# A fused hybrid layer on one core: projections loaded and turned in thirds, the two folds in a row, another order of the attention stage

## Chip, core and metric

One core of one Trainium2 chip. The metric is the device time of one execution in microseconds; the median of three executions is 124.89 us (124.87 to 124.93). The core's engines are TensorE (PE; its weight loads are listed as PEld), VectorE (DVE), ScalarE (ACT), GpSimd (POOL) and SyncE (SP), which here only issues DMAs. Each works through its own queue in order and they meet only through semaphores.

## The reference, cut to what matters

The input x is 2 x 512 x 256, float32. Four blocks follow one another, each with a residual:

```python
x = x + attn_a(layernorm(x), qkv, o_proj, gamma, beta)   # itself: layernorm * gamma + beta, q, k, v,
                                                         # causal softmax(q k^T / 16) v, o_proj, + residual
x = x + ffn(layernorm(x), gate_w, up_w, down_w, scales)  # weights rounded to fp8; silu(gate) * up, then down
x = x + s4d(layernorm(x), D, log_dt, A, C)               # a convolution over 512 steps with a complex kernel
x = x + ffn(layernorm(x), ...)                           # the same weights again
```

## The kernel before

The 1024 rows of x are eight tiles of 128 rows: tiles 0 to 3 are the first batch, 4 to 7 the second. The program is one hand-written list per engine; there is no planner, and the order in each list is the order of the work.

**The opening, 0 to about 28 us.** TensorE fills its time with transposes of the identity matrix (`warm_up`, 14 of them, L1099), turns the q third of `qkv` when it has landed (`turn_w`, L1107), does 8 more identity transposes, and turns the k third. It turns the parameter rows (L1148), turns the first two normalised tiles (`turn_z`, L1122), and multiplies the turned q and k thirds into one 256x256 matrix `wqk` (`fold`, L1114). It turns tiles 2 and 3 and the v third, and makes g = xn wqk for the whole first batch (`make_g`, L1131: eight passes of 512 columns). Only then comes the second fold, `wvo` = v o_proj, then the turning of the second batch, v rows for the first batch (`make_v`, L1138: sixteen passes of 256 columns), `scores(0)` (L1173), the turning of the scales (L1230), `make_g(1)`, `scores(1)`, `turn_probs(0)` (L1186) and `make_v(1)`.

Each product has to be copied from PSUM before TensorE can use it: ScalarE copies the turned thirds (L505), `wqk` and `wvo`, and half of xn, g and v; VectorE the other half. xn needs gamma and beta, which `params` holds, read by VectorE from the turned parameter rows. `normed` is made by VectorE for the first batch (L739) and by ScalarE for the second (L540); the reciprocal standard deviations are GpSimd's (L296, L301, L306).

ScalarE's list also has one tanh and one sine group for the convolution's taps, the squares of the gate and up weights (L558) and the exponentials. An activation of another table set is preceded by an ACT_TABLE_LOAD.

**Attention, to 51.9 us.** For k = 2 to 7, TensorE does `scores(k)`, `attend(k-2)` (L1198), `turn_probs(k-1)`. VectorE takes each row maximum (L892), ScalarE the exponential (L578) and the copy of the turned probabilities (L586), VectorE the division and residual (L900) and the statistics. Between these stand VectorE's work on the three fp8 grids (L811, L816) and on the down weights (`lift_down`, `lower_down`), and GpSimd's rounding of the gate and up weights (`round_weight`, L413 and L416), the factors of x_plus (`x_plus_scales`, L400 to L404), the reciprocal deviations of the new x, the first and middle part of the taps, and the six tiles of `down16` (L446).

**Four passes of the feed-forward part.** In each, TensorE does 6 steps `gate_up(n, m)` (L1258) and, three steps later, `down(n, m)` (L1292); `spread_taps` (L1303) stands in pass 0 after step 4, and `copy_taps` (L629) on ScalarE brings its result to SBUF before `turn_h(1, 0)` may write the same PSUM bank.

**DMA order on SP (L243 to L256):** x tiles 0-1, q, x tiles 2-3, k, four parameter rows, v, x tiles 4-5, 6-7, o_proj, two scale rows, gate, up, down, down_scale. ScalarE issues three small loads, GpSimd two (c_re, c_im).

Of the kernel before, what the change touches and what calls it, by code (L numbers as in the profile page):

```python
# [34 lines left out]
WARM_UP = 14  # L35
WARM_BETWEEN = 8
# [9 lines left out]
def hybrid_layer(nc, x, qkv, o_proj, gamma, beta, d_param, log_dt, a_real_log, a_imag, c_re, c_im,  # L46
# [13 lines left out]
    with ctx:  # L60
# [48 lines left out]
        param_rows = sb("param_rows", [4 * C, P])  # L109
        params = sb("params", [P, 4 * C])  # L110
        gammas, betas, log_dts, d_params = (params[:, C * n:C * n + C] for n in range(4))
# [33 lines left out]
        q_loaded, k_loaded, v_loaded, wo_loaded = sem("q_loaded"), sem("k_loaded"), sem("v_loaded"), sem("wo_loaded")  # L145
# [83 lines left out]
        def _(sp):  # L229
# [25 lines left out]
            load_chunks(down_raw[:], down_w, w_loaded[2])  # L255
            sp.dma_start(down_scale_all[:], down_scale.partition_broadcast(P)).then_inc(down_scale_loaded, 16)  # L256
# [16 lines left out]
        def _(pool):  # L273
# [11 lines left out]

            def load_s4d(n, array, loaded):
                pool.dma_start(s4d_in[:, n, :].rearrange("p (c n) -> p c n", c=C),
                               array.rearrange("(c p) n -> p c n", p=P)).then_inc(loaded, 16)
# [97 lines left out]
            def constants():  # L386

                load_s4d(2, c_re, c_loaded)
                load_s4d(3, c_im, c_loaded)
# [58 lines left out]
            inverse_std(1, T, 2, negative_mean=True)  # L448
            taps_middle()
            inverse_std(1, T + 2, 2, negative_mean=True)  # L450
            taps_end()
# [18 lines left out]
            for n in range(2 * B):  # L470
# [19 lines left out]
                else:  # L490
                    tail(n, POOL_TAILS[n][0])
                    if n == 3:
# [9 lines left out]
        def _(act):  # L502
            def turned(w):
# [4 lines left out]
            def xn_chunk(b):  # L508
                act.wait_ge(params_ready, 1)
                act.wait_ge(z_turned, C * b + 1)  # L510
                act.activation(xn_cols[:, b, 0, :], psum[:, BANK_Z[b][0], :], ACT.Identity, scale=gammas[:, 0:1],
                               bias=betas[:, 0:1]).then_inc(xn_by_act, 1)

            def g_part(b):
                act.wait_ge(g_made, C * b + 1)
                act.activation(g_cols[:, b, 0, :], psum[:, BANK_G[b][0], :], ACT.Copy,
# [6 lines left out]

            act.dma_start(e_in[:, 0:HN].rearrange("p (c n) -> p c n", c=C),
# [9 lines left out]
            act.wait_ge(wqk_made, 1)  # L534
            act.activation(wqk[:].rearrange("p c n -> p (c n)"), psum[:, BANK_WQK, :], ACT.Copy).then_inc(wqk_ready, 1)
            xn_chunk(0)
            turned(2)
# [4 lines left out]
            act.wait_ge(wvo_made, 1)  # L542
# [828 lines left out]
```

## Time and profile before

| | |
|---|---|
| median of 3 runs | 124.89 us (124.87 to 124.93) |
| the profiled execution | 124.83 us, of which the span from first to last instruction is 123.0 us |
| PE busy | 116.2 us, 94% of the span |
| DVE, POOL, ACT busy | 96.1, 83.7, 77.5 us |
| granted TensorE clock, mean | 0.995 |

The page lists busy time by engine; the chain of waits follows the work back from the last instruction; a timeline lists instructions in order of time, each with the idle time of its engine before it and what ended that. Every number of the argument is from the one profiled execution. A matmul's listed duration holds its way through the array; the next one of an unbroken row starts earlier than it ends. A float32 matmul is listed as two passes.

### The profile page before, as it was taken

What the parts mean: (1) busy time and instruction counts of PE and PEld (TensorE: products, weight loads), DVE (VectorE), ACT (ScalarE), POOL (GpSimd) and SP (SyncE); (2) the same over time, 40 slices, a digit from 0 to 9 for tenths busy, and PEclk for the clock granted to TensorE, in tenths of its full rate; (3) what the DMA queues carried; (4) which work ended last, traced back from release to release, by engine and by line L of the source; (5) the groups of instructions that cost most, each with busy time, mean ns of one, the idle gap of its engine ahead of it and who ended that gap; (6) DMA issues with size and microseconds to landing.
All of it is one profiled execution on the core that took longest, in us unless ns stands there. A gap on an engine that the chain in (4) does not pass through costs nothing.

```text
span 123.0 us, 2126 instructions
## 1 busy us (share of the span) xinstructions
PE 116.2 (94%) x682; PEld 78.3 (64%) x682; DVE 96.1 (78%) x229; ACT 77.5 (63%) x147; POOL 83.7 (68%) x165
## 2 busy tenths in 40 slices
PE   5997999999999999999999999999999999999970
PEld 5885468658668758744678645667445479756650
DVE  0499999919865878768797988999899994797582
ACT  2235079695776367947966359786389666589700
POOL 2246569999999888888633388869876782037721
PEclk9999999999999999999999999999999999999997
DMA  3999930000000000000000000000000000000505
GB/s 94 302 308 365 337 101 8 0 0 0 0 0 0 3 8 0 0 0 0 0 0 0 5 0 0 0 3 5 0 0 0 3 0 5 0 0 0 171 0 171
DMA packets 5682, 5.80 MB, mean 47 GB/s; under 512 B 1140, under 2 KB 5160, under 8 KB 5672
## 3 DMA queue, kind: packets, MB, share of 16 engines
q1 hardware_dynamic: 4648, 5.52, 13.5%
q10 hardware_dynamic: 960, 0.15, 0.7%
q8 instruction: 5, 0.08, 0.3%
q0 software_dynamic: 64, 0.02, 0.2%
q14 instruction: 5, 0.04, 0.1%
HBM read 4.63 MB, written 1.05 MB: 46 GB/s over the span
## 4 chain that ended last, share of the span: by engine, by line
PE 60%; DVE 18%; POOL 7%; ACT 6%; issue 3%; DMA 2%; POOLq 0%; DVEq 0%; ACTq 0%
PE psum L1258 18%; PE psum L1292 10%; PE psum L1198 7%; PE psum L1173 7%; PE psum L1138 6%; DVE stats L731 5%; PE psum L1131 3%; PE psum L1272 3%; POOL rstd L301 3%; PE psum L1220 2%; DMA x_in<-in_x 2%; PE psum L1186 2%; DVE x_plus L974 2%; ACT h_rows L570 2%; DVE fused L1005 2%
## 5 line engine op out<-in xcount | busy, mean ns | idle before, releaser
L619 ACT ACTIVATE gated<-psum,scales 128x512 f32<-128x512 f32 x24 | 16.3, 681 | 12.4 <-PE psum L1258 10.2
L1292 PE MATMUL psum<-down,f_head 128*128 128x256 bf16 x96 | 22.0, 273 | 0.0
L1292 PE MATMUL psum<-down,f_tail 128*128 128x256 bf16 x96 | 22.0, 273 | 0.0
L1005 DVE SCALAR_TENSOR_TENSOR fused<-psum,up_scales_fit,gated 128x512 f32<-128x512 f32 (+1 forms) x25 | 17.8, 716 | 3.5 <-PE psum L1258 2.3
L456 POOL TENSOR_TENSOR f_tail<-fused,f_head 128x512 f16<-128x512 f32 x10 | 11.8, 1184 | 11.8 <-ACT f_head L625 10.6
L625 ACT ACTIVATE f_head<-fused 128x512 f16<-128x512 f32 (+1 forms) x25 | 15.2, 607 | 2.6 <-DVE fused L1005 2.3
L1013 DVE TENSOR_TENSOR f_tail<-fused,f_head 128x512 f16<-128x512 f32 (+1 forms) x15 | 10.2, 680 | 4.2 <-ACT f_head L625 4.2
L1258 PE MATMUL psum<-h_tail,gate 128*128 128x512 f16 x44 | 13.1, 379 | 0.0
L1258 PE MATMUL psum<-h_head,gate 128*128 128x512 f16 x44 | 13.1, 379 | 0.0
L1258 PE MATMUL psum<-h_tail,up 128*128 128x512 f16 x44 | 13.1, 379 | 0.0
L1258 PE MATMUL psum<-h_head,up 128*128 128x512 f16 x44 | 13.1, 379 | 0.0
L301 POOL TENSOR_TENSOR rstd<-var_eps,neg_half 128x2 f32<-128x2 f32 (+1 forms) x15 | 11.4, 759 | 2.2
L1292 PEld LDWEIGHTS psum<-down,f_head 128*128 128x128 f16 x96 | 9.4, 98 | 3.2 <-DVE f_tail L1013 0.9
L1198 PE MATMUL psum<-v_rows,probs_cols 128*128 128x256 f32 x40 | 10.3, 389 | 0.2 <-ACT probs_cols L586 0.2
L1292 PEld LDWEIGHTS psum<-down,f_tail 128*128 128x128 f16 x96 | 9.4, 98 | 1.8
L1173 PE MATMUL psum<-xn_cols,g_cols 128*128 128x128 f32 (+3 forms) x32 | 10.0, 436 | 0.0
L296 POOL TENSOR_SCALAR var_eps<-mean_var 128x2 f32<-128x2 f32 (+1 forms) x15 | 3.8, 256 | 8.6 <-DVE mean_var L734 7.7
L1198 PEld LDWEIGHTS psum<-v_rows,probs_cols 128*128 128x128 f32 x40 | 7.0, 190 | 2.3 <-ACT probs_cols L586 0.8
L1131 PE MATMUL psum<-xn_cols,wqk 128*128 128x512 f32 x16 | 7.4, 603 | 0.8 <-DVE xn_cols L750 0.8
L462 POOL TENSOR_TENSOR x<-scaled_down,x 128x256 f32<-128x256 f32 x8 | 5.6, 727 | 3.2 <-DVE scaled_down L957 3.2
L462 POOL TENSOR_TENSOR x_in<-scaled_down,x_plus 128x256 f32<-128x256 f32 x6 | 4.8, 810 | 4.3 <-DVE scaled_down L957 2.9
L1258 PEld LDWEIGHTS psum<-h_tail,gate 128*128 128x128 f16 x44 | 4.2, 98 | 5.3 <-DVE h_tail L887 0.6
(176 smaller groups left out, 265.1 us busy)
## 6 DMA issues: line engine op xcount, KB each, us to landing
x_in<-in_x SPq DMA_DIRECT2D x4, 256.0 KB, 4.4
qkv_sb<-in_qkv SPq DMA_DIRECT2D x3, 256.0 KB, 4.3
gate_raw<-in_gate_w SPq DMA_DIRECT2D x1, 768.0 KB, 6.3
up_raw<-in_up_w SPq DMA_DIRECT2D x1, 768.0 KB, 8.1
down_raw<-in_down_w SPq DMA_DIRECT2D x1, 768.0 KB, 9.7
out<-x_in SPq DMA_DIRECT2D x3, 256.0 KB, 2.1
wo_sb<-in_o_proj SPq DMA_DIRECT2D x1, 256.0 KB, 5.0
down_scale_all<-in_down_scale SPq DMA_DIRECT2D x1, 128.0 KB, 9.6
```

What stands on the lines that cost most here:

```text
L301: power = pool.tensor_tensor(rstd[:, n, k:k + count], var_eps[:, n, k:k + count], neg_half[:, 0:count], ALU.pow)
L456: pool.tensor_tensor(f_tail[:, m, :], fused[:, m % FUSED, :], f_head[:, m, :], ALU.subtract).then_inc(f_tail_by_pool, 1)
L462: pool.tensor_tensor(new[:, k, :], scaled_down[:, k, :], old[:, k, :], ALU.add).then_inc(ready, 1)
L619: act.activation(gated[:, m % 2, :], psum[:, BANK_GATE[m % 2], :], ACT.Silu, scale=gate_scales[:, m:m + 1]).then_inc(gated_ready, 1)
L625: act.activation(f_head[:, m, cols], fused[:, m % FUSED, cols], ACT.Copy).then_inc(f_head_ready, 1)
L1005: dve.scalar_tensor_tensor(out=fused[:, m % FUSED, cols], in0=psum[:, BANK_UP[m % 2], cols], scalar=up_scales_fit[:, m:m + 1], in1=gated[: ...
L1013: dve.tensor_tensor(f_tail[:, m, cols], fused[:, m % FUSED, cols], f_head[:, m, cols], ALU.subtract).then_inc(f_tail_by_dve, 1)
L1131: last = pe.matmul(column(BANK_G[b][j], 0, S), wqk[:, c, j * P:j * P + P], xn_cols[:, b, c, :], start=(c == 0), stop=(c == C - 1))
L1173: pe.matmul(column(BANK_S[k % 2], 0, W), g_cols[:, b, j, i * P:i * P + P], xn_cols[:, b, j, 0:W], start=(j == 0), stop=(j == C - 1))
L1198: last = pe.matmul(column(BANK_O[k % 2], 0, H), probs_cols[:, k % 2, t * P:t * P + P], v_rows[:, b, t, :], start=(t == 0), stop=(t == i))
L1258: last = pe.matmul(column(banks[m % 2], 0, S), w[:, c, m * P:m * P + P], part[:, c, :], start=(part is h_head and c == 0), stop=(part is h ...
L1292: last = pe.matmul(down_columns(n, t), part[:, m, t * P:t * P + P], down16[:, m, :], start=(m == 0 and (t % 2 == 0 or n == 2 * B - 1) and ...
```

## The change

- SP loads the three thirds of `qkv` directly behind x tiles 0-1, then x tiles 2-3 and `o_proj`. The log_dt row is no longer among the parameter rows, and the three that remain are issued by ScalarE ahead of its own loads. c_re and c_im move from GpSimd's queue to the end of SP's.
- TensorE: 9 identity transposes instead of 14, none between q and k; the three thirds are turned in a row; the folds `wqk` and `wvo` stand in a row; xn, g and v of the first batch are made in halves of 256 rows; `scores(0)` and `scores(1)` stand before the second half of g; `make_v(0)`'s second half and `make_g(1)` follow. At the end `attend(6)` stands before `turn_probs(7)`.
- The banks of `wvo` and of the first g change to fit this.
- ScalarE: `turned(2)` in a row with the others, xn, g and v as above, the tanh and sine group behind the first square, `exp_scores(0)` and `(1)` together; for k = 3, 6, 7 `copy_probs(k-1)` stands before `exp_scores(k)`; `copy_taps` stands behind `gate(0, 5)`.
- VectorE: another order of the same operations, with xn and g in halves. GpSimd: `x_plus_scales` before `round_weight(0)`, two `inverse_std` earlier, `taps_end` behind the first tail of pass 0; `spread_taps` stands after step 5.

```diff
-WARM_UP = 14
-WARM_BETWEEN = 8
+WARM_UP = 9
...
-        BANK_WT, BANK_WQK, BANK_WVO, BANK_PARAMS, BANK_SCALES, BANK_NORMS = [4, 5, 3], 2, 3, 7, 4, 5
+        BANK_WT, BANK_WQK, BANK_WVO, BANK_PARAMS, BANK_SCALES, BANK_NORMS = [4, 5, 3], 2, 4, 7, 4, 5
-        BANK_G = [[6, 7], [0, 1]]
+        BANK_G = [[5, 2], [0, 1]]
...
             load_x(0)
-            load_chunks(qkv_sb[:, :, 0:KEY], qkv[:, 0:KEY], q_loaded)
+            for w in range(3):
+                load_chunks(qkv_sb[:, :, w * KEY:(w + 1) * KEY], qkv[:, w * KEY:(w + 1) * KEY], w_qkv_loaded[w])
             load_x(1)
-            load_chunks(qkv_sb[:, :, KEY:2 * KEY], qkv[:, KEY:2 * KEY], k_loaded)
-            load_rows(param_rows, (gamma, beta, log_dt, d_param), params_loaded)
-            load_chunks(qkv_sb[:, :, 2 * KEY:], qkv[:, 2 * KEY:], v_loaded)
+            load_chunks(wo_sb[:], o_proj, wo_loaded)
             load_x(2)
             load_x(3)
-            load_chunks(wo_sb[:], o_proj, wo_loaded)
...
             inverse_std(0, T, T, twice=True, negative_mean=True)
+            x_plus_scales()
             round_weight(0, gate16, gate_up_ready)
-            x_plus_scales()
             angle_squares()
             round_weight(1, up16, gate_up_ready)
             inverse_std(1, 0, 2, negative_mean=True)
             taps_begin()
+            inverse_std(1, 2, 2, negative_mean=True)
             pool.wait_ge(bound_squared, 1)
...
-            inverse_std(1, 2, 2, negative_mean=True)
+            inverse_std(1, T, 2, negative_mean=True)
...
+            load_row(0, gamma)
+            load_row(1, beta)
+            load_row(2, d_param)
...
             turned(0)
             turned(1)
+            turned(2)
+            xn_half(0)
+            act.wait_ge(wqk_made, 1)
+            act.activation(wqk[:].rearrange("p c n -> p (c n)"), psum[:, BANK_WQK, :], ACT.Copy).then_inc(wqk_ready, 1)
+            act.wait_ge(wvo_made, 1)
+            act.activation(wvo[:].rearrange("p c n -> p (c n)"), psum[:, BANK_WVO, :], ACT.Copy).then_inc(wvo_ready, 1)
+            g_first_half()
             act.wait_ge(tanh_in, 1)
             act.activation(s4d[:, 3, :], s4d[:, 2, :], ACT.Tanh, scale=0.5).then_inc(tanh_out, 1)
...
+            xn_half(1)
             for k in range(T, K):
                 act.wait_ge(shift_ready[0], k - T + 1)
...
+                if k == T:
+                    v_part(0)
+
+            xn_second()
...
             square_weights(0)
+            trig()
+            copy_scales()
             exp_scores(0)
-            g_part(1)
+            exp_scores(1)
+            g_part()
             square_weights(1)
-            exp_scores(1)
             copy_probs(0)
             v_part(1)
...
-                exp_scores(k)
-                copy_probs(k - 1)
+                if k in (3, 6, 7):
+                    copy_probs(k - 1)
+                    exp_scores(k)
+                else:
+                    exp_scores(k)
+                    copy_probs(k - 1)
...
-                else:
+                gate(n, 5)
+                if n == 0:
                     copy_taps()
-                gate(n, 5)
...
+            xn_half(1)
             grid_begin(0)
             grid_end(0)
-            g_chunk(0)
+            exp_finish()
+            exp_times_dt()
+            g_second_half()
+            xn_second()
+            reduce_angle()
+            row_max(0)
+            row_max(1)
             grid_begin(1)
...
+            def make_g_half(half):
+
+                columns_there(half + 1)
                 for j in range(C):
                     for c in range(C):
+                        last = pe.matmul(column(BANK_G[0][half], j * (S // 2), S // 2), wqk[:, c, j * P:j * P + P],
+                                         xn_cols[:, 0, c, HALVES[half]], start=(c == 0), stop=(c == C - 1))
+                last.then_inc(g_made, 1)
...
+            turn_w(0)
+            turn_w(1)
+            turn_w(2)
+
+            pe.wait_ge(params_loaded, 48)
+            pe.transpose(column(BANK_PARAMS, 0, 3 * C), param_rows[:], ident[0:3 * C, 0:3 * C]).then_inc(params_turned, 1)
+            turn_z_half(0)
             pe.wait_ge(w_turned_ready, 2)
             fold(BANK_WQK, 0, lambda kc: w_turned[:, 1, kc, :]).then_inc(wqk_made, 1)
-            turn_z(0, (2, 3))
-            turn_w(2, v_loaded)
-            pe.wait_ge(wqk_ready, 1)
-            pe.wait_ge(params_ready, 1)
-            make_g(0)
             pe.wait_ge(w_turned_ready, 3)
             pe.wait_ge(wo_loaded, 16)
             fold(BANK_WVO, 2, lambda kc: wo_sb[:, kc, :]).then_inc(wvo_made, 1)
+            pe.wait_ge(wqk_ready, 1)
+            make_g_half(0)
+            turn_z_half(1)
+            pe.wait_ge(wvo_ready, 1)
+            make_v(0, (0, 1))
...
-            turn_z(1)
-            pe.wait_ge(wvo_ready, 1)
-            make_v(0)
             scores(0)
-
+            scores(1)
+            pe.wait_ge(v_by_act, 1)
+            make_g_half(1)
+            turn_z()
+            make_v(0, (2, 3))
+
+            columns_there(3)
             pe.wait_ge(scales_loaded, 32)
-            pe.wait_ge(xn_by_act, 2)
             pe.transpose(column(BANK_SCALES, 0, 2 * M), scale_rows[:], ident[0:2 * M, 0:2 * M]).then_inc(scales_turned, 1)
-            make_g(1)
-            scores(1)
+            make_g()
             turn_probs(0)
...
+            attend(K - 2)
             turn_probs(K - 1)
-            attend(K - 2)
             turn_h(0, 1, first=True)
...
-                    if n == 0 and m == 4:
+                    if n == 0 and m == M - 1:
                         spread_taps()
```

## Rows read from the trace of the kernel before

**Rows 1.** The page: busy time of the engines; granted clock in 40 slices.
```profile
PE 116.2 (94%) x682; PEld 78.3 (64%) x682; DVE 96.1 (78%) x229; ACT 77.5 (63%) x147; POOL 83.7 (68%) x165
PEclk9999999999999999999999999999999999999997
```
**Rows 2.** Windows: stretch, its length, busy time of each engine, clock, DMA share, GB/s.
```profile
0.00:11.59 11.59, 9.26 (x51) 7.93 (x52) 6.35 (x25) 4.34 (x7) 5.16 (x19) 1.00 0.83 262
...
27.55:51.85 24.30, 24.07 (x139) 18.27 (x138) 18.80 (x55) 16.48 (x39) 22.16 (x46) 1.00 0.00 1
51.85:123.02 71.17, 67.07 (x435) 42.12 (x433) 57.89 (x123) 46.27 (x84) 43.76 (x91) 0.99 0.05 16
```
**Rows 3.** Timeline of PE, opening: start, duration, instruction, count, idle before and releaser.
```profile
1.52 3.25 PE L1099 MATMUL psum<-ident 128*128 128x128 f32 x14 [1.52 <-POOL ident L282]
4.76 1.06 PE L1107 MATMUL psum<-ident,qkv_sb 128*128 128x128 f32 x4
5.66 1.04 PE L1099 MATMUL psum<-ident 128*128 128x128 f32 x8
6.57 0.66 PE L1107 MATMUL psum<-ident,qkv_sb 128*128 128x128 f32 x4
...
7.91 1.99 PE L1114 MATMUL psum<-w_turned 128*128 128x256 f32 x8
9.74 0.60 PE L1122 MATMUL psum<-ident,normed 128*128 128x128 f32 x4
10.18 0.60 PE L1107 MATMUL psum<-ident,qkv_sb 128*128 128x128 f32 x4
11.59 0.67 PE L1131 MATMUL psum<-xn_cols,wqk 128*128 128x512 f32 x1 [0.81 <-DVE xn_cols L750]
```
**Rows 4.** Chain of waits, in order of time: start, length, what.
```profile
15.23 0.80 POOL neg_mean_rstd L306
...
16.06 2.08 ACT normed L540 x4
```
**Rows 5.** Loads of the thirds: issue to landing of the three; k's issue.
```profile
DMA to landing us min/median/max: 3.5/4.3/4.5
2.23 0.47 SPq L234 DMA_DIRECT2D qkv_sb<-in_qkv  x1
```
**Rows 6.** Timeline of PE, 22.9 to 32 us.
```profile
22.98 3.70 PE L1131 MATMUL psum<-xn_cols,wqk 128*128 128x512 f32 x8
...
27.55 3.62 PE L1138 MATMUL psum<-wvo,xn_cols 128*128 128x256 f32 x16
```
**Rows 7.** Groups by line and shape, 4 to 52 us: count, busy us, mean ns, idle before.
```profile
L558 ACT ACTIVATE square<-gate_raw 128x1536 bf16<-128x1536 f32 x1 | 1.5, 1477 | 0.0
L511 ACT ACTIVATE xn_cols<-psum,params 128x512 f32<-128x512 f32 x2 | 1.5, 768 | 0.0
L549 ACT ACT_TABLE_LOAD x1 | 1.3, 1283 | 0.0
...
L549 ACT ACTIVATE s4d<-s4d 128x16 f32<-128x16 f32 x1 | 0.2, 218 | 0.0
L578 ACT ACTIVATE probs<-psum,neg_max 128x128 f32<-128x128 f32 x2 | 0.7, 368 | 0.0
L586 ACT ACTIVATE probs_cols<-psum 128x512 f32<-128x512 f32 x2 | 1.2, 586 | 1.2 <-PE psum L1186 1.2
```
**Rows 8.** Timeline of PE, attention: its one long wait, and the end.
```profile
36.97 1.56 PE L1198 MATMUL psum<-v_rows,probs_cols 128*128 128x256 f32 x6 [0.23 <-ACT probs_cols L586]
...
48.39 1.46 PE L1198 MATMUL psum<-v_rows,probs_cols 128*128 128x256 f32 x6
49.69 0.60 PE L1220 MATMUL psum<-ident,h_rows 128*128 128x128 f32 x4
```
**Rows 9.** Timeline of POOL and ACT: the last rounding, the taps.
```profile
36.23 3.74 POOL L416 TENSOR_TENSOR up<-scaled_down,grid 128x512 f16<-128x512 f32 x3
62.51 0.60 ACT L629 ACTIVATE taps_all<-psum 128x512 f32<-128x512 f32 x1
```

More of the change, by code:

```diff
@@ L108, in hybrid_layer @@
         pos_half = sb("pos_half", [P, M])
-        param_rows = sb("param_rows", [4 * C, P])
-        params = sb("params", [P, 4 * C])
-        gammas, betas, log_dts, d_params = (params[:, C * n:C * n + C] for n in range(4))
+        param_rows = sb("param_rows", [3 * C, P])
+        params = sb("params", [P, 3 * C])
+        gammas, betas, d_params = (params[:, C * n:C * n + C] for n in range(3))
         scale_rows = sb("scale_rows", [2 * M, P])
@@ L255, in _ @@
             load_chunks(down_raw[:], down_w, w_loaded[2])
+            for n, array in ((2, c_re), (3, c_im)):
+                load_chunks(s4d_in[:, n, :].rearrange("p (c n) -> p c n", c=C), array, c_loaded)
             sp.dma_start(down_scale_all[:], down_scale.partition_broadcast(P)).then_inc(down_scale_loaded, 16)
@@ L541, in _, with trig, copy_scales @@
                                bias=neg_mean_rstd[:, 0, k:k + 1]).then_inc(z_by_act, 1)
[L542 to L553 removed]
+                if k == T:
+                    v_part(0)
+            xn_second()
+            def trig():
+                act.wait_ge(trig_in, 1)
+                act.activation(s4d[:, 10, 0:HN], s4d[:, 8, 0:HN], ACT.Tanh, scale=0.5)
+                act.activation(s4d[:, 11, 0:HN], s4d[:, 9, 0:HN], ACT.Sin)
+                act.activation(s4d[:, 12, 0:HN], s4d[:, 9, 0:HN], ACT.Sin, scale=0.5).then_inc(trig_out, 1)
+            def copy_scales():
+                act.wait_ge(scales_turned, 1)
+                act.activation(scales[:], psum[:, BANK_SCALES, 0:2 * M], ACT.Copy).then_inc(scales_ready, 1)
             def square_weights(w):
@@ L1101, in _, with turn_w @@
             warm_up(WARM_UP)
-            def turn_w(w, loaded):
-                pe.wait_ge(loaded, 16)
+            def turn_w(w):
+                pe.wait_ge(w_qkv_loaded[w], 16)
                 for kc in range(C):
@@ L1116, in fold, with turn_z, turn_z_half, columns_there @@
                 return last
-            def turn_z(b, tiles=range(T)):
-                for t in tiles:
-                    pe.wait_ge(z_by_act if b else z_ready, t + 1)
+            def turn_z():
+                for t in range(T):
+                    pe.wait_ge(z_by_act, t + 1)
                     for c in range(C):
-                        turned = pe.transpose(column(BANK_Z[b][c], t * P, P), normed[:, T * b + t, c * P:c * P + P], ident[:])
+                        turned = pe.transpose(column(BANK_Z[1][c], t * P, P), normed[:, T + t, c * P:c * P + P], ident[:])
                         if t == T - 1:
                             turned.then_inc(z_turned, 1)
-            def make_g(b):
-                pe.wait_ge(xn_by_act, b + 1)
-                pe.wait_ge(xn_by_dve, b + 1)
+            def turn_z_half(half):
+                for t in (2 * half, 2 * half + 1):
+                    pe.wait_ge(z_ready, t + 1)
+                    for c in range(C):
+                        last = pe.transpose(column(BANK_Z[0][c], t * P, P),
+                                            normed[:, t, c * P:c * P + P], ident[:])
+                last.then_inc(z_turned, 1)
+            def columns_there(made):
+                pe.wait_ge(xn_by_act, made)
+                pe.wait_ge(xn_by_dve, made)
+            def make_g_half(half):
+                columns_there(half + 1)
                 for j in range(C):
                     for c in range(C):
-                        last = pe.matmul(column(BANK_G[b][j], 0, S), wqk[:, c, j * P:j * P + P], xn_cols[:, b, c, :],
+                        last = pe.matmul(column(BANK_G[0][half], j * (S // 2), S // 2), wqk[:, c, j * P:j * P + P],
+                                         xn_cols[:, 0, c, HALVES[half]], start=(c == 0), stop=(c == C - 1))
+                last.then_inc(g_made, 1)
+            def make_g():
+                for j in range(C):
+                    for c in range(C):
+                        last = pe.matmul(column(BANK_G[1][j], 0, S), wqk[:, c, j * P:j * P + P], xn_cols[:, 1, c, :],
                                          start=(c == 0), stop=(c == C - 1))
                     last.then_inc(g_made, 1)
-            def make_v(b):
-                for t in range(T):
+            def make_v(b, tiles=range(T)):
+                for t in tiles:
                     for c in range(C):
```

136 lines of the change are left out of this document (67 added, 69 removed).

## The prediction

> **What bounds the kernel now.** I read the page first. TensorE is busy 94% of the span, and its granted clock stays in the top tenth until the last slice [rows 1]. Then windows. From the first matmul of pass 0 at 51.85 us to the end, TensorE is busy 67.1 of 71.2 us, and in attention 24.07 of 24.30 us [rows 2]. The other engines have 5 to 13 us free in each of those stretches. So from about 18.7 us on every microsecond is TensorE's, and a saving in the opening reaches the end unchanged unless a new wait stands in between.
>
> The opening is where TensorE waits, or works for nothing. In its timeline [rows 3] it makes 8 idle transposes between q and k, waits 0.81 us for VectorE's half of xn, and reaches g only at 11.59. The chain of waits shows the second hole: GpSimd's reciprocal deviations end at 16.03 and ScalarE needs until 18.14 for four tiles of the second batch [rows 4]. TensorE turns each as it comes, 0.88 us of work in about 1.8 us, and then waits for `wvo`.
>
> **The new opening.** The v third is issued fourth, in k's old place at 2.23. Issue to landing took 4.3 us in the middle of the three thirds [rows 5], so v lands near 6.5, where now it has to be issued behind four parameter rows and TensorE reaches it at 10.18 [rows 3]. x tiles 2-3 come one place later; their product z is wanted only at 12.8. From v's landing, TensorE has these pieces. A pass of 256 columns is 0.216 us ((3.62 - 0.38) / 15, [rows 6]), a block of eight 1.73; a transpose 0.11 (0.44 for four, 9.74 to 10.18 in [rows 3]); `make_g` at full width 3.54 (22.98 to 26.52).
>
> - Six blocks of eight (two folds, two halves of g, two of v): 10.38.
> - 20 transposes (v third, first batch, second batch): 2.20, and 0.10 for a first one that waited.
> - Parameter and scale rows: 0.25. `scores(0)` and `(1)`: four passes of 128 and four of 256 columns and two masks, 1.42.
> - `make_g(1)`: 3.54.
>
> The sum is 17.89; from 6.57 it ends at 24.46, and `turn_probs(0)` could start. Now that one ends at 27.55, so it starts at 27.44: a gain of 2.98, if nothing waits. I followed the copies: the `wqk` copy is ready at 10.2 for a use at 11.1, xn at 8.4 for 11.1, the first half of v at 16.0 for 16.4, the last normalised tile at 17.5 for 18.8. These waits cost nothing; the thinnest cover is v's 0.4, which depends on GpSimd's deviations being ready by about 15.0.
>
> **One wait opens.** ScalarE gets the second batch's columns at 19.24 (6.57 plus 12.47 of the pieces above, plus 0.2 for the crossing). Behind them stand xn 0.66, the square of the gate weights 1.48, a table load 1.28 for the sines, the tanh, sines and scales 0.53 together, another table load 1.28, and the first exponential 0.36 [rows 7]. That is 5.59, so the probabilities are there at 24.9 instead of 24.46. TensorE waits 0.4, and restarting costs it another 0.1, as at 36.97 [rows 8]: `make_v(1)` starts near 25.1 against 27.55. Gain so far 2.45.
>
> **Attention.** The passes are the same. The wait at 36.97 for `probs_cols` [rows 8] was 0.39 with the restart behind it; the reordered copy leaves about 0.22, gain 0.17. Two waits come in at the end. `attend(6)` now stands directly behind `turn_h(0, 0)`, 0.44 long, and needs a copy that starts after `turn_probs(6)`: 0.20 crossing, 0.37 copy, 0.10 back, against 0.44 cover: 0.29 late with what remains of ScalarE's order. `attend(7)` stands behind `turn_probs(7)` and `turn_h(0, 1)`; it needs the copy of 512 columns (0.49 of the 586 ns [rows 7] before the next may start), where in the kernel before `attend(6)` [rows 8], 1.30 long, covered it: 0.41 late. With 0.1 for each restart that is 0.9 lost. The old order also waited 0.1 before `turn_probs(7)`, gone. Net of attention: -0.17 - 0.1 + 0.9 = +0.6.
>
> **What hides the rest.** GpSimd: `x_plus_scales`, now first, delays `round_weight(0)`, but the start is 2 us earlier because the deviations need not wait for the parameter work on VectorE; by the durations of before both weights are rounded near 37, and pass 0 starts near 50. Now the last rounding ends at 39.97 [rows 9]. If that cover went, the cost would be at most what exceeds 13 us. The two DMAs taken from GpSimd save it 1.7 us of a wait. `down16` ends near 51.5, used at 57. `copy_taps` ends near 63.7 and `turn_h(1, 0)` wants the bank at 63.8: cover 0.1, bounds 0 and 0.6 (the copy itself [rows 9]); I take 0. The three small loads on ScalarE's queue end its issuing near 3.8 instead of 2.3, the table load then near 5.1, and its first copy is wanted at 5.86: nothing.
>
> **Sum.** 2.45 - 0.6 = 1.85. The same addition made for the old order ends its attention 0.26 too early against the trace, so it is short of small crossings; against that addition the new order gains 1.6. I take 1.7. The profiled execution took 124.83 us, of which the span is 123.0, and lies 0.06 under the median: 124.89 - 1.7 = **123.2 us**. Bounds from the same pieces: the new waits absent, a gain of 2.5 (122.4); each twice as long, 0.9 (124.0).
>
> **The unknown: the granted clock.** The listed clock is 1.00 throughout, but the spacing tells more [rows 3]: 14 transposes take 3.25 us and the four of q start 0.22 apart (the 1.2 GHz level), the 8 from 5.66 on 0.11 apart (2.4 GHz). The clock rose about 4.1 us after TensorE's first transpose, all that time filled. Now there are 9 transposes, done at 3.5; a hole of 1.2 us follows before q lands. If the clock still rises near 5.7 nothing is lost, since TensorE waits for k and v. Its other bound: the 4.1 us count anew from 4.76, so it rises at 8.9. From 6.57 on half speed costs half the time, 1.2 us. I take the first, as the row shows work spread over the same time, but not safely.
>
> The Trainium skill, "TensorE: Matmul & The Clock Gate", Part 4, says that work in transpose mode does not count as busy for the clock as matmuls do. The rows show the clock rising with transposes alone before it, so the trace disagrees. By that rule it would start from the first fold, a rival below.
>
> **The rivals.**
> - *Late clock (8.9).* For: the hole of 1.2 us. Against: TensorE has been working half of the time before. Gain 1.7 - 1.2 = 0.5: 124.4.
> - *Very late clock, the slower one.* Only the folds, from 7.7 on, raise it, 4.1 us later at 11.8; place: thirds, folds and first g at half speed; price 5.2 / 2 = 2.6: 125.8. It decides from a rise at about 10.0 on, where half of the time since 6.57 equals 1.7. For: the clock now rose only after 4.1 us of unbroken work, and the page's rule. Against: [rows 3].
> - *Reordered queues bound attention.* ScalarE and VectorE have long fixed rows (grids, down weights) between row maxima; if contention delays `row_max(2)` or the last three by 0.4 each, 1.2 to 1.6 is lost: 124.6. For: VectorE's grid operations and GpSimd's rounding overlap in another way. Against: 5.5 us of VectorE's time in attention is free [rows 2].
> - *The load order does nothing:* v lands as late as 8.5 behind the small loads' packets, 2.0 lost: 125.2. Against: k's landing in the same place.
>
> **How the numbers follow.** Forecast 0.56 (own range 122.4 to 124.0); late clock 0.20; queues 0.12; very late clock 0.07; late v 0.05. Range over the first three: 122.4 to 124.8. A change under 0.2% (0.25 us) can't be told from none. Faster: 0.56 + 0.17 + 0.08 = 0.81; same: 0.03 + 0.04 = 0.07; slower: 0.07 + 0.05 = 0.12.
>
> **What would show it.** Right: v's transposes near 6.6 at 0.11 apart, `make_g_half(0)` near 11.1, no TensorE wait until about 24.5, `make_v(1)` at 25.1, pass 0 at 50.1. Wrong: transposes of k and v 0.22 apart (clock), a wait for `v_rows` at 16.4, a wait above 0.5 before `turn_probs(0)`, or TensorE waiting in pass 0.

## The result, and the profile after

The changed kernel takes 132.69 us median (131.24 to 133.04, 4 runs) beside 124.91 us (124.87 to 125.14) for the kernel before on the same chip: a ratio of 1.059 with a 95% interval of 1.055 to 1.064. The forecast was 123.2 us, range 122.4 to 124.8. It was wrong by 9.5 us and in direction. The profiled execution took 132.91 us, its span 131.1 us.

Medians and ranges below are over all runs of a kernel, but a ratio leaves out runs more than 1.5% above that kernel's fastest (so in runs 4 and 6 it is smaller than the medians say), and none is given where that would leave one run of four (1, 3 and 7).

The page after: busy time of each engine, and the granted clock in 40 slices. They answer to [rows 1].

```profile
PE 118.8 (91%) x677; PEld 81.3 (62%) x677; DVE 98.2 (75%) x230; ACT 77.9 (59%) x148; POOL 82.7 (63%) x163
PEclk9999999997579999999999999999999999999998
```

A dip of the clock in the tenth to twelfth slice is new. Windows of the same execution, cut at `make_v(1)` and at the first matmul of pass 0, with two more around the dip; the columns are those of [rows 2].

```profile
27.10:32.20 5.10, 0.47 (x3) 0.33 (x3) 5.07 (x8) 4.01 (x11) 3.42 (x6) 0.89 0.00 0
32.20:38.50 6.30, 6.30 (x18) 5.06 (x18) 1.24 (x2) 4.66 (x9) 6.22 (x6) 0.54 0.00 0
...
32.14:59.95 27.81, 27.34 (x139) 20.39 (x138) 18.21 (x52) 17.07 (x40) 19.27 (x36) 0.90 0.00 1
59.95:131.10 71.15, 67.04 (x435) 42.16 (x433) 58.40 (x125) 46.17 (x84) 44.70 (x92) 0.99 0.05 16
```

Pass 0 to the end takes 71.15 us, as before [rows 2]. All 8.1 us lie ahead of it: 59.95 against 51.85. They fall into four parts (which add up to 0.6 more, mainly because `scores(1)`, 0.9 us, no longer stands behind `make_g(1)`).

TensorE's timeline of the changed kernel, its opening and the place of the long wait (start, duration, instruction, count, idle before it and releaser), against [rows 3] and [rows 6]:

```profile
4.32 1.12 PE L1152 MATMUL psum<-ident,qkv_sb 128*128 128x128 f32 x4 [0.63 <-DMA qkv_sb<-in_qkv]
6.38 2.10 PE L1152 MATMUL psum<-ident,qkv_sb 128*128 128x128 f32 x8 [0.95 <-DMA qkv_sb<-in_qkv]
...
9.52 2.45 PE L1159 MATMUL psum<-w_turned 128*128 128x256 f32 x8
11.80 1.89 PE L1159 MATMUL psum<-wo_sb,w_turned 128*128 128x256 f32 x8
...
31.87 0.47 PE L1253 MATMUL psum<-ident,probs 128*128 128x128 f32 x1 [4.63 <-ACT probs L597]
```

1. **The opening is late.** The eight transposes of k and v take 2.10 us, the 1.2 GHz level; before, those of k took 0.66 for four [rows 3]. The record of the clock rises at 10.64 us (before: 5.65). `make_g(1)` starts at 23.54, not at 20.92 as forecast: 2.6 us later than forecast, 0.6 later than before.
2. **TensorE waits 4.63 us** for the first probabilities.
3. **The clock falls** at 31.12, in that wait, and rises at 37.95: the window above shows 0.54, and `make_v(1)` takes 6.3 us instead of 3.5.
4. **Attention** without that loss is 24.93 us (27.81 - 2.88) instead of 24.30: 0.6 longer, as forecast.

What stands behind the wait is in VectorE's and GpSimd's timelines of the same stretch:

```profile
21.76 0.81 DVE L784 TENSOR_SCALAR xn_cols<-psum,params 128x512 f32<-128x512 f32 x1
22.49 0.58 DVE L835 TENSOR_SCALAR s4d<-s4d 128x16 f32<-128x16 f32 x1
23.10 1.19 DVE L836 TENSOR_SCALAR s4d<-s4d 128x16 f32<-128x16 f32 x1
24.33 2.56 DVE L838 SCALAR_TENSOR_TENSOR s4d<-s4d 128x16 f32<-128x16 f32 x3
26.93 1.19 DVE L839 TENSOR_SCALAR s4d<-s4d 128x16 f32<-128x16 f32 x1
```
```profile
20.53 3.73 POOL L407 TENSOR_TENSOR x<-gate_raw,grid 128x512 f32<-128x512 f32 x3
24.34 3.74 POOL L410 TENSOR_TENSOR gate<-x,grid 128x512 f16<-128x512 f32 x3
```

The six steps of `reduce_angle` work on 16 columns. In the kernel before they ran from 13.86 to 15.12, 0.17 to 0.20 each, ahead of the gate grid, with rounding starting at 17.04:

```profile
13.86 0.17 DVE L796 TENSOR_SCALAR s4d<-s4d 128x16 f32<-128x16 f32 x1
14.07 0.20 DVE L797 TENSOR_SCALAR s4d<-s4d 128x16 f32<-128x16 f32 x1
14.30 0.59 DVE L799 SCALAR_TENSOR_TENSOR s4d<-s4d 128x16 f32<-128x16 f32 x3
14.93 0.19 DVE L800 TENSOR_SCALAR s4d<-s4d 128x16 f32<-128x16 f32 x1
...
16.00 0.96 DVE L816 TENSOR_SCALAR grid<-grid 128x1536 f32<-128x1536 f32 x1
...
21.00 2.02 DVE L811 TENSOR_SCALAR grid<-down_raw 128x1536 uint32<-128x1536 uint32 x1
```

In the changed kernel they take 5.6 us, and five of the six are stretched. The stretched ones end 0.02 to 0.04 us after a rounding piece of 1.26 to 1.30 us ends; the short one (0.18) fell into GpSimd's pause at 24.3. The copy of xn from PSUM, just ahead and also beside rounding, takes 0.81, the kernel before's 0.80 at 19.06. The last line above is a sign that the trace of before already held: a VectorE grid step took 2.02 us beside rounding where its like took 0.96 alone.

ScalarE gets the angles at 28.14 and then needs two table loads before the first exponential:

```profile
28.14 0.22 ACT L566 ACTIVATE s4d<-s4d 128x16 f32<-128x16 f32 x1 [4.35 <-DVE s4d L839]
28.37 1.28 ACT L567 ACT_TABLE_LOAD   x1
...
30.07 1.28 ACT L597 ACT_TABLE_LOAD   x1
31.36 0.37 ACT L597 ACTIVATE probs<-psum,neg_max 128x128 f32<-128x128 f32 x1
```

**Theories.** P: a VectorE step on SBUF operands waits out the GpSimd step that is running on SBUF, so a chain of tiny steps beside rounding costs 1.2 us a link. C: the clock is a second cost, in the opening (gaps between the loads) and behind the long wait. Rivals: the place of the steps in the queue alone (Q, with ScalarE's tables); attention bound by the reordered queues.

### The profile page after: what moved, and what is told of

The parts are those of the page before. It is cut to its first block, busy times and chain, and to the rows that moved or that the text cites. A ratio compares the mean times of both kernels' runs of the same rounds, so it can differ in the third digit from the quotient of the medians.

```text
span 131.1 us, 2118 instructions
## 1 busy us (share of the span) xinstructions
PE 118.8 (91%) x677; PEld 81.3 (62%) x677; DVE 98.2 (75%) x230; ACT 77.9 (59%) x148; POOL 82.7 (63%) x163
## 3 DMA queue, kind: packets, MB, share of 16 engines
HBM read 4.63 MB, written 1.05 MB: 43 GB/s over the span
## 4 chain that ended last, share of the span: by engine, by line
PE 63%; DVE 16%; ACT 8%; POOL 4%; DMA 4%; issue 3%; SPq 1%; POOLq 0%; DVEq 0%
PE psum L1326 16%; PE psum L1360 10%; PE psum L1265 7%; PE psum L1240 6%; PE psum L1203 6%; DMA qkv_sb<-in_qkv 4%; PE psum L1159 3%; PE psum L1340 3%; PE psum L1189 3%; DVE stats L756 2%; PE psum L1253 2%; DVE s4d L838 2%; DVE x_plus L1019 2%; ACT h_rows L589 2%; DVE fused L1050 2%
## 5 line engine op out<-in xcount | busy, mean ns | idle before, releaser
L292 POOL TENSOR_SCALAR var_eps<-mean_var 128x2 f32<-128x2 f32 (+1 forms) x15 | 4.4, 295 | 17.8 <-DVE mean_var L759 17.0
L1203 PE MATMUL psum<-wvo,xn_cols 128*128 128x256 f32 x32 | 10.3, 487 | 0.0
L931 DVE TENSOR_REDUCE neg_max<-psum 128x1 f32<-128x128 f32 (+3 forms) x8 | 3.7, 476 | 7.2 <-PE psum L1242 7.1
L1203 PEld LDWEIGHTS psum<-wvo,xn_cols 128*128 128x128 f32 x32 | 8.1, 260 | 1.5
L1253 PE MATMUL psum<-ident,probs 128*128 128x128 f32 x20 | 3.7, 283 | 4.6 <-ACT probs L597 4.6
```

Of the source, the lines that this page charges most:

```text
L1203: last = pe.matmul(column(BANK_V[b][t // 2], H * (t % 2), H), xn_cols[:, b, c, t * P:t * P + P], wvo[:, c, :], start=(c == 0), stop=(c == ...
L1253: last = pe.transpose(column(BANK_PT[k % 2], t * P, P), probs[:, k % 2, t * P:t * P + P], ident[:])
```

## The experiments

Medians are given with that of the kernel before from the same job. "v1" is the start of `make_v(1)`, "p0" of pass 0, in the profiled execution (before: 27.55 and 51.85; after: 32.14 and 59.95).

**1. The angle steps earlier in VectorE's queue**

```diff
             exp_times_dt()
+            reduce_angle()
             g_second_half()
             xn_second()
-            reduce_angle()
```

> The changed kernel with one line moved on VectorE: reduce_angle directly behind exp_times_dt, ahead of g_second_half, so it begins near 19.8 us, before GpSimd's rounding of the gate weights begins (20.5), instead of at 22.5, beside it. Theory P (overlap): each of its six 16-column operations took about 1.2 us because a GpSimd operation on SBUF was running; alone they take 1.2 us together. So trig_in comes near 21 to 22, the first exponential near 27.3, TensorE waits 0.3 instead of 4.6 before turn_probs(0), its clock does not fall, make_v(1) takes 3.5 instead of 6.3: 132.9 - 4.3 - 2.9 = 125.7. Rival Q (ScalarE's order with two table loads and the square behind the second batch is the cause): less than 1 us is won, 132.

Measured: 132.49 us median, but runs of 132.63, 132.34, 133.54 and 125.31, before 125.17. The median is rival Q's number, but not for Q's reason: in the profiled one rounding had started by 19.8, and the steps of `exp_times_dt` were caught as well:

```profile
19.82 1.20 DVE L829 TENSOR_SCALAR s4d<-s4d 128x8 f32<-128x8 f32 x1
20.94 1.32 DVE L830 TENSOR_SCALAR s4d<-s4d_in,s4d 128x8 f32<-128x8 f32 x1
22.17 1.31 DVE L829 TENSOR_SCALAR s4d<-s4d 128x8 f32<-128x8 f32 x1
23.40 0.22 DVE L830 TENSOR_SCALAR s4d<-s4d_in,s4d 128x8 f32<-128x8 f32 x1
23.65 1.19 DVE L835 TENSOR_SCALAR s4d<-s4d 128x16 f32<-128x16 f32 x1
...
27.82 0.69 DVE L789 TENSOR_SCALAR g_cols<-psum 128x512 f32<-128x512 f32 x1
```

The stretch moved with the rounding, not with the steps, and now `xn_second` stood behind it: TensorE waited 5.2 us before `make_g(1)`. One run of four took 7 us less, near the 125.7 that P gave; it has no profile, so that it escaped the overlap is inferred. The ten tiny steps of the two groups are in a race with GpSimd's start.

**2. and 3. Fourteen idle transposes ahead of q, as before; alone, and with edit 1**

```diff
-WARM_UP = 9
+WARM_UP = 14
```

> The changed kernel with 14 identity transposes at the start instead of 9, nothing else. Rival C (the clock's late rise at 10.6 us is the main cause): below 129. Theory P: the opening gains about 1.6 us (the folds run at full clock from near 8.4), but the wait for the exponential is set by GpSimd's rounding beside reduce_angle and takes most of it back: 0.5 to 1.6 us won, 131.3 to 132.4.

> Both: reduce_angle early and 14 identity transposes. P with the clock's rise near 5.7: 125.7 less 1.6 = 124.1. If the early rise is worth nothing: the same as with reduce_angle early alone, 125.7.

Measured: 131.53 us (131.50 to 132.06), a ratio of 1.052 (1.048 to 1.055); and 132.35 with one run of 124.62. The clock rose at 5.28, fell again at 8.70 and rose at 12.11 (run 2). TensorE's timeline shows why the opening gained nothing: 1.3 us idle before k.

```profile
6.83 0.66 PE L1152 MATMUL psum<-ident,qkv_sb 128*128 128x128 f32 x4 [1.32 <-DMA qkv_sb<-in_qkv]
...
9.14 3.36 PE L1159 MATMUL psum<-w_turned 128*128 128x256 f32 x8
```

The eight passes of the fold take 3.36 us, before 1.99 [rows 3]. More transposes in front do not replace the ones between the loads. That run 2 lies in its forecast range is luck: the opening was to give 1.6 us, but `make_g(1)` starts 1.6 later (25.16 against 23.54), as three steps of `exp_times_dt` were caught here too (19.68 to 23.35). What came back is in the wait (2.89 instead of 4.63) and in the second dip of the clock, which ended at 36.00, so that `make_v(1)` took 5.1 us instead of 6.3. Run 3 repeats the race of run 1.

**4. Rounding waits for the angles**

```diff
+            pool.wait_ge(trig_in, 1)
             round_weight(0, gate16, gate_up_ready)
```

> The changed kernel with GpSimd's round_weight(0) waiting for the end of reduce_angle (trig_in); VectorE's order is that of the changed kernel. P: the six operations take 1.2 us together in their late place, trig_in near 23.7, first exponential near 27.3, TensorE waits 0.3: 125.7; GpSimd's delay of 3 us is hidden. A rival in which the late place in VectorE's list is the cause, not the overlap: nothing won, 132.

Measured: 128.87 us (128.33 to 130.84), a ratio of 1.028 (1.024 to 1.032). VectorE's timeline:

```profile
22.84 0.17 DVE L836 TENSOR_SCALAR s4d<-s4d 128x16 f32<-128x16 f32 x1
23.04 0.17 DVE L837 TENSOR_SCALAR s4d<-s4d 128x16 f32<-128x16 f32 x1
23.25 0.60 DVE L839 SCALAR_TENSOR_TENSOR s4d<-s4d 128x16 f32<-128x16 f32 x3
23.88 0.18 DVE L840 TENSOR_SCALAR s4d<-s4d 128x16 f32<-128x16 f32 x1
```

With nothing changed in the steps or their place, they take 1.2 us instead of 5.6: P is shown, and the place in the queue is ruled out. v1 was 27.99, the clock did not fall. The forecast 125.7 was missed all the same: attention then took 27.4 us (p0 55.39), 2.5 more than in the changed kernel without its slow `make_v(1)`, which I had not expected. Rounding started at 24.14, 3.6 us later, and met VectorE's grids; GpSimd's deviations for the output rows came late:

```profile
24.14 5.15 POOL L407 TENSOR_TENSOR x<-gate_raw,grid 128x512 f32<-128x512 f32 x3 [4.70 <-DVE s4d L840]
...
44.41 0.78 POOL L292 TENSOR_SCALAR var_eps<-mean_var 128x2 f32<-128x2 f32 x1
```
```profile
53.08 0.65 PE L1288 MATMUL psum<-ident,h_rows 128*128 128x128 f32 x4 [2.04 <-ACT h_rows L590]
```

So GpSimd's start has a limit on both sides: too early it blocks the small steps, too late it binds attention.

**5. The kernel before, with its angle steps beside rounding**

```diff
-            reduce_angle()
             grid_begin(0)
             grid_end(0)
             g_chunk(0)
+            reduce_angle()
```

> The kernel before with one thing changed: the six 16-column steps of the angle reduction stand behind grid_begin(0), grid_end(0) and g_chunk(0), so that they meet GpSimd's rounding, which there starts at 17.0 us. Theory P (each small VectorE step on SBUF waits out the 1.27 us GpSimd operation that is running): the six steps take 6 to 7 us instead of 1.3, trig_in comes at 23 to 25 instead of 15.1, ScalarE's chain of tables puts the first probabilities near 28, TensorE waits 1 to 4 us before turn_probs(0), and where it waits over 2 us the clock may fall: 126.5 to 131 us. Rival (the size of the delay comes from the place in the queue alone, each step still 0.2 us): trig_in near 19.5, no wait, 125 us.

Measured: 126.68 us (126.30 to 126.82) beside 124.98, a ratio of 1.012 (1.009 to 1.015).

```profile
16.94 1.12 DVE L796 TENSOR_SCALAR s4d<-s4d 128x16 f32<-128x16 f32 x1
18.10 1.19 DVE L797 TENSOR_SCALAR s4d<-s4d 128x16 f32<-128x16 f32 x1
19.33 2.58 DVE L799 SCALAR_TENSOR_TENSOR s4d<-s4d 128x16 f32<-128x16 f32 x3
21.94 1.19 DVE L800 TENSOR_SCALAR s4d<-s4d 128x16 f32<-128x16 f32 x1
```

The same six steps are stretched in the other kernel too, 6.2 us, with the angles at 23.1 as P said. It cost less, and elsewhere than I expected: TensorE waits 1.02 us for `xn_cols` before `make_g(1)`, none before `turn_probs(0)`. v1 is 29.40, 1.85 later; in this execution 0.65 of that was there at the first g already (12.24 against 11.59; its clock rose at 7.34), so the chain's own part here is about 1.2. The price depends on what stands behind the chain.

**6. TensorE kept at work through the wait**

```diff
             make_g()
+            warm_up(40)
             turn_probs(0)
```

> The changed kernel with 40 idle identity transposes between make_g(1) and turn_probs(0), 4.4 us at full clock, just as long as TensorE waited there. Theory C (the fall of the granted clock behind the wait is a cost of its own, 2.9 us): make_v(1) takes 3.5 us instead of 6.3 and the time falls to about 130.0; the wait itself stays 4.6 us in another form. Rival (the slow make_v(1) has another reason, such as its operands): nothing changes, 132.7.

Measured: 131.78 us (129.76 to 132.57), a ratio of 1.044 (1.035 to 1.054).

```profile
28.80 4.53 PE L1144 MATMUL psum<-ident 128*128 128x128 f32 x40
33.17 0.27 PE L1253 MATMUL psum<-ident,probs 128*128 128x128 f32 x1
33.28 3.62 PE L1203 MATMUL psum<-wvo,xn_cols 128*128 128x256 f32 x16
```

The clock stays up and `make_v(1)` takes 3.6 us: the fall is shown to be a cost of its own. Only 0.9 of the 2.9 us showed in the median, as the filling itself ended some 1.4 us behind the first exponential (31.70), and this execution's `make_g(1)` came 1.7 later: three steps of `exp_times_dt` met rounding (19.80 to 23.45) and held up xn. Up to there the program is that of the changed kernel, so the race of run 1 is in it too.

**7. All small steps ahead of the gate grid**

```diff
-            grid_begin(0)
-            grid_end(0)
             exp_finish()
             exp_times_dt()
+            reduce_angle()
+            grid_begin(0)
+            grid_end(0)
             g_second_half()
             xn_second()
-            reduce_angle()
```

> The changed kernel with VectorE's order exp_finish, exp_times_dt, reduce_angle, then grid_begin(0), grid_end(0), g_second_half, xn_second. All small steps now stand before the grid, and GpSimd's rounding cannot start before the grid's end, so nothing small meets it; rounding starts near 21.0 instead of 20.5, so unlike the run in which rounding waited for the angle GpSimd is hardly later. Theory P: every small step 0.2 us, trig_in near 19, the wait before turn_probs(0) 0.3 to 0.6, no fall of the clock: make_v(1) near 27.8, 125.3 to 126.2 us, and the same in every run. Rival (the queues of attention are the loss, whatever the opening does): 128 and more.

Measured: 126.40 us (123.66 to 127.27) beside 124.98. 6.3 us come back, to 0.2 above the forecast range. No small step is stretched, v1 is 28.88 where I had 27.8. The runs still lie 3.6 us apart, and in the profiled one the clock rose at 12.75 and the first fold started at 10.03.

**8. The same, the opening filled**

```diff
+            warm_up(12, 6)
             turn_w(1)
+            warm_up(4, 6)
             turn_w(2)
+            warm_up(2, 6)
```

with 14 idle transposes ahead of q; the second argument is the PSUM bank that they write, one that nothing reads in the opening.

> The changed kernel with VectorE's small steps ahead of the gate grid, as in the run before (126.40 us median, 123.66 to 127.27, with the clock rising at 12.75 in its profiled execution and the first fold at 10.03), and with the opening's gaps filled: 14 idle transposes ahead of q, 12 between q and k, 4 between k and v, 2 behind v. Theory C (late and varying rise of the clock in the opening): it rises near 5.3 and stays, the first fold starts near 8.5 at full clock, 1.0 to 2.5 us is gained on the median and the runs lie within 0.6 us: 123.8 to 125.2. Rival (the opening is bound by landings and copies): under 0.3 gained, the same spread.

Measured: 125.08 us (124.14 to 125.39, 10 runs) beside 124.93, a ratio of 1.000 (0.997 to 1.002). The clock rises at 6.19 and stays; 1.3 us are gained, the spread falls from 3.6 to 1.25. v1 is 27.12, p0 52.07. The first fold starts only at 9.62, though:

```profile
7.30 0.66 PE L1152 MATMUL psum<-ident,qkv_sb 128*128 128x128 f32 x4
7.79 0.60 PE L1144 MATMUL psum<-ident 128*128 128x128 f32 x4
8.23 0.60 PE L1152 MATMUL psum<-ident,qkv_sb 128*128 128x128 f32 x4
...
9.62 1.25 PE L1159 MATMUL psum<-w_turned 128*128 128x256 f32 x5
```

v's last packet landed at 8.10 here and at 7.33 in the changed kernel. I had put it at 6.5.

**9. and 10. Sines ahead of `xn_second`; and the end of attention undone.** Run 9 is run 8 with `trig()` ahead of ScalarE's `xn_second()` and VectorE's order grid_begin(0), small steps, xn_second, grid_end(0), g_second_half. Run 10 adds the diff of run 12 below.

> As the one before, with ScalarE's tanh and sines (one table load) ahead of xn_second, where ScalarE stood idle for 1.9 us, and VectorE's order grid_begin(0), small steps, xn_second, grid_end(0), g_second_half. Theory Q (the two table loads behind xn_second make the first probabilities late, which costs 0.3 to 0.4): the wait before turn_probs(0) goes, 123.3 to 124.6, at least 0.3 less than the one before if there the wait shows. Rival (moved work delays xn_second's ScalarE half, or rounding later than 21.5 costs more in attention): no gain.

> As the one before, with the end of attention as in the kernel before the change: ScalarE's exp_scores(k) always ahead of copy_probs(k-1), turn_probs(7) ahead of attend(6). By my prediction the changed order cost 0.6 us in attention, so undoing it gives 0.4 to 0.7 us: 122.8 to 124.0. Rival (the 0.6 us of the changed kernel came from its late rounding and stretched VectorE steps, not from the order): no difference, within 0.2 us.

Measured: 128.37 us (127.39 to 129.02), a ratio of 1.025 (1.019 to 1.031); and 126.87, 1.016 (1.013 to 1.020). The wait before `turn_probs(0)` is gone (v1 at 27.15), but p0 is 56.03. The row of run 4 is back: rounding starts at 23.49, and TensorE waits 2.58 us for `h_rows` at 52.38. In that wait the clock falls (51.92, until 55.33), and what stands from there to pass 0 takes 3.65 us where run 4 needs 2.31. The second side of GpSimd's limit, hit by my own order. Run 10 can't speak of the order of attention, since GpSimd bounds both.

**11. The kernel before, its opening unfilled**

```diff
-WARM_UP = 14
-WARM_BETWEEN = 8
+WARM_UP = 9
+WARM_BETWEEN = 0
```

> The kernel before with 9 idle transposes instead of 14 and none between q and k, nothing else changed. Theory C: the clock rises later than 5.65, between 8.9 and 12.8, and what stands before it at half clock (k, two batches' transposes, folds, g) takes up to twice as long, of which waits hide a part: 0.5 to 2.0 us slower, 125.5 to 127.0. Rival (the opening waits for its operands anyway): 124.9.

Measured: 126.58 us (126.21 to 126.65) beside 124.93, a ratio of 1.012 (1.010 to 1.014). The clock rises at 10.83 instead of 5.65, v1 is 29.30. The 13 removed transposes compute nothing and are worth 1.65 us.

**12. Run 8 with the end of attention as before**

```diff
-                if k in (3, 6, 7):
-                    copy_probs(k - 1)
-                    exp_scores(k)
-                else:
-                    exp_scores(k)
-                    copy_probs(k - 1)
+                exp_scores(k)
+                copy_probs(k - 1)
...
-            attend(K - 2)
             turn_probs(K - 1)
+            attend(K - 2)
```

> The version that tied with the kernel before (VectorE's small steps ahead of the gate grid, the opening filled: 125.08 us median; its profiled execution has make_v(1) at 27.13 and pass 0 at 52.08, 24.95 apart, where the kernel before has 24.30), with the end of attention as before the change: exp_scores(k) always ahead of copy_probs(k-1), turn_probs(7) ahead of attend(6). By my prediction's term the changed order costs 0.6 us: 124.3 to 124.7, pass 0 at 24.3 behind make_v(1). Rival (the 0.65 us are GpSimd's and VectorE's, later by 3.8 us than in the kernel before, when rounding starts): no gain, or a loss where a copy is late: 124.9 to 125.7.

Measured: 124.36 us (123.78 to 124.69) beside 125.07, a ratio of 0.994 (0.992 to 0.996), 0.6% under run 8's. It is ahead of both kernels, of the kernel before by only 0.6%. Its profile is less clear than its median: v1 26.82, p0 51.59, so attention is 24.77 us, 0.2 less than in run 8 and not the 24.3 expected, for two other waits are there:

```profile
36.36 0.92 PE L1264 MATMUL psum<-v_rows,probs_cols 128*128 128x256 f32 x3 [0.34 <-ACT probs_cols L605]
...
47.63 0.66 PE L1252 MATMUL psum<-ident,probs 128*128 128x128 f32 x4 [0.26 <-ACT probs L597]
```

Run 15 was made to decide.

**13. and 14. Small steps in VectorE's first idle time, tables early; and one piece of the new order of attention put back** (`copy_probs(2)` ahead of `exp_scores(3)`).

> The one before, with VectorE's exp_reduce in its idle time ahead of copy_params (8.3 to 9.2), exp_finish ahead of the last statistics, and ScalarE's tanh behind its first half of xn, its sines ahead of xn_second. Theory P: still no small step meets a rounding step; the gate grid ends and rounding starts about 1.3 us sooner (19.4 instead of 20.8), and the 0.34 us before turn_probs(0) go. 0.3 to 1.2 us less than the one before: 123.3 to 124.4. Rival (ScalarE's wait for the sines, or a VectorE step late for xn_half, opens another wait): no gain or up to 1 us slower.

> The version with all small steps and tables early and the end of attention as before the change (124.25 us in its undisturbed runs), with one piece of the change's attention order put back: copy_probs(2) ahead of exp_scores(3). By my prediction's term that takes 0.17 us off the wait of 0.34 us that attend(2) has there: 124.0 to 124.2. Rival (exp_scores(3) later by a copy makes turn_probs(3) late by the same): 124.25 to 124.5.

Measured: 124.31 us (five runs of 123.73 to 124.69; the profiled one took 140.10 at a granted clock of 0.85, and its rows are not used), a ratio of 0.993 (0.991 to 0.996); and 124.36 (123.83 to 124.89), a ratio of 0.995 (0.993 to 0.997). Neither differs from run 12. Run 14 was to give 124.0 to 124.2: in its profile the wait at `attend(2)` is gone, which starts it 0.27 earlier behind v1 than in run 12, but attention as a whole is 24.86 long, so nothing is left of it. In run 14's profile rounding starts at 20.28, no sooner than run 12's 20.40: `x_plus_scales` ahead of it holds GpSimd, so the freed VectorE time reached nothing.

**15. The kernel before, with the new order of attention alone** (the diff of run 12 the other way round)

> The kernel before with the change's order of attention alone: copy_probs(k-1) ahead of exp_scores(k) for k = 3, 6, 7, attend(6) ahead of turn_probs(7). My prediction's term: -0.17 - 0.1 + 0.9 = 0.6 us slower, 125.3 to 125.7 beside 125.0. Rival (that loss belongs to the later rounding): within 0.2 us of before.

Measured: 125.58 us (125.45 to 126.25) beside 124.96, a ratio of 1.005 (1.003 to 1.007). In its profile attention takes 24.94 us (27.67 to 52.61) against 24.30, and the two waits that I had forecast are there: `attend(6)` starts 0.30 us and `attend(7)` 0.41 us later than behind unbroken work, while `attend(2)` starts 0.14 earlier. The lines of `attend(6)` and `attend(7)`:

```profile
48.09 1.56 PE L1202 MATMUL psum<-v_rows,probs_cols 128*128 128x256 f32 x6
...
50.78 1.99 PE L1202 MATMUL psum<-v_rows,probs_cols 128*128 128x256 f32 x8 [0.25 <-ACT probs_cols L586]
```

Six more profiled executions with the new order and rounding not late (runs 1, 2, 3, 6, 7, 8; run 2 without what its slow `make_v(1)` lost) take 24.9 to 25.0 us for attention as well, at v1 from 27.12 to 34.75.

## Why the prediction was wrong

Pass 0 was forecast at 50.1 and came at 59.95, 9.8 us later:

| | us |
|---|---|
| the opening: v later, clock at the 1.2 GHz level until 10.64 | 2.6 |
| wait before `turn_probs(0)`: 4.63 instead of about 0.5, with crossings | 4.4 |
| clock fallen behind it, `make_v(1)` | 2.9 |
| attention, beyond the forecast 0.6 | 0 |

**The step that failed first is "One wait opens".** It followed ScalarE's row from xn to the exponential and took the angles as being there. It priced VectorE's six steps at nothing and never laid them beside GpSimd's rounding, which may start once the gate grid has ended and did so at 20.53, behind `x_plus_scales`. In the kernel before the steps ended at 15.12 and the grid at 16.96: they did not overlap. The change's VectorE order puts grid first and steps last. Runs 4 and 7 remove the overlap in two ways and get 3.8 and 6.3 us back; run 5 makes it in the other kernel. The rule was to be had: the Trainium skill, "SBUF — State Buffer", section "Who interferes with whom", says that VectorE and GpSimd contend for one shared port pair as an exclusive lock. It limits this to VectorE instructions in a mode that uses both ports or with two inputs in SBUF, and says that the one that comes second is blocked for the whole of the other. The rows here agree for these steps beside rounding, and disagree for steps of the same kinds beside GpSimd's powers (last section); in which mode the steps with one input ran, no row shows.

**A reading of the rows was wrong beside it.** "The other engines have 5 to 13 us free in each of those stretches" does not hold for GpSimd: in attention it is busy 22.16 of 24.30 us [rows 2], 2.1 free. So a later start of rounding had less room than the sentence gives, which runs 4 and 9 met.

**The clock was mis-sized, and its fall in the wait not seen.** I gave a rise near 5.7 more than half of the chance. It rose at 10.64 to 12.75 in six of the profiled unfilled openings, or rose at about 5 and fell again (runs 2 and 3). The "late" and "very late clock" rivals, 1.2 and 2.6 us, were right in kind; run 11 prices it at 1.65 us for the kernel before. That the clock would fall in a long wait was in no step, since no long wait was.

**v did not land at 6.5.** Taking k's old place in the queue gave it another time: 7.33 in the changed kernel, 6.80 (run 4) to 8.10 (run 8) in the others with the new load order. Why is open: as many bytes stand ahead of v as stood ahead of k, but a third of the weights in place of x tiles 2-3, and ScalarE's three parameter rows are issued beside them; no run separates these. With the opening filled the pieces that I had summed to 17.89 us from v's transposes on take about 18.6 (8.23 to 26.78 in run 8, 7.92 to 26.48 in run 12), 0.3 of which are the two idle transposes behind v. So their sum was 0.4 short, and their start 1.35 to 1.7 us late. What is left of the forecast 2.45 us is 0.7 (v1 at 26.82 in run 12 against 27.55).

**Attention's 0.6 was right,** by place and size (run 15: 0.64 us in its profile, `attend(6)` 0.30 and `attend(7)` 0.41 late where I had 0.29 and 0.41, and 0.5% in the median; run 12 against 8: 0.6% in the medians, of which their profiles show 0.2 us in attention and 0.3 in the opening). The rival "reordered queues" named VectorE's and GpSimd's overlap, but looked for it in attention at 0.4 us a piece; it was ahead of it, at 1.2 us a link of a chain.

**"What hides the rest"** held for weights and taps. It missed that rounding's start also has a latest time, and that seems to count from `make_v(1)`: starting 3.7 to 3.9 us ahead of v1 (24.14, 23.49 and 22.60 in runs 4, 9 and 10) attention lost 2.5, 3.9 and 2.8 us against the same order in the changed kernel, run 8 and run 12 (1.3 of the 3.9 to the fallen clock), 6.4 to 6.6 ahead of it (22.41, 20.76, 20.40 and 20.28 in runs 7, 8, 12 and 14) nothing of that kind. Where between the two the limit lies, no run shows.

## What to carry to other kernels

Price a small step not by its own duration but by the step of the other engine that it may have to wait for (here rounding pieces of 1.27 us), once for every link of its chain, and lay the two engines' rows side by side before moving either. Idle work between loads is part of the design: take it out only with a row at hand that shows the clock level without it. Where a kernel's runs spread over 2 us or more, look for a race between two engines' orders, and end it with an order in which one can't start before the other is done.

## What the runs showed that I had not expected

- Not every step is blocked. GpSimd's powers on 8 columns (2.38 us long in the changed kernel, 17.45 to 19.83) did not stretch VectorE's small steps at 18.22 to 19.79, each 0.17 to 0.27, while rounding pieces of 1.27 did. The same in run 7: the powers at 17.37, 1.65 long there, VectorE's steps beside them 0.17 to 0.27. VectorE's steps that read PSUM kept their durations (xn 0.81).
- It goes both ways. A grid of 1536 columns takes 0.95 us alone and up to 2.03 beside rounding, and a rounding piece then 1.98 instead of 1.27 (run 4). GpSimd's own small steps on 16 columns take 0.91 to 0.96 us beside VectorE's grids in the changed kernel (30.07 to 32.91), where two of them took 0.20 before (31.81, 31.97).
- Identity transposes raise the clock ([rows 3]: 5.65) and hold it (run 6: 40 of them, no fall until the end), and with a gap of 1.32 us before k the clock rose at 5.28 and fell again at 8.70 (run 2).
